# A fused decoder layer on one core: two steps of the attention loop reordered, experts' loads and scatters released differently

## What is computed

```
x = x + attention(layernorm(x))       # rmsnorm * norm_w; 16 heads of 64, causal softmax, sigmoid gate per head, out projection
x = x + retention(layernorm(x), ctx)  # 16 heads of 8: q from x, k = v = ctx, position-rotated, decay mask, no softmax
x = x + experts(layernorm(x))         # 12 experts, top 3 per token, softmax over the 3 logits
                                      # h = gelu(x Wup + bup), 128 -> 512; y = h Wdown + bdown, 512 -> 128
```

## Time and profile before

| | |
|---|---|
| median of 3 runs | 562.97 us (560.76 to 564.37) |
| profiled execution, its own time | 557.62 us |
| its span in the trace | 555.8 us |
| PE busy | 482.0 us, 87% |
| DVE busy | 393.8 us, 71% |
| ACT busy | 340.4 us, 61% |
| POOL busy | 281.2 us, 51% |
| chain that ended last | PE 46%, DVE 19%, issue 10%, ACT 10%, unknown 5% |

### The profile page before, as it was taken

One profiled execution on the slowest core, in us unless ns is written; L12 is line 12 of the kernel. 1 busy time (PEld: TensorE's weight loads), 2 busy tenths in 40 slices (PEclk: granted clock), 3 DMA queues, 4 the chain that ended last, 5 costly groups with the idle time before them and its releaser, 6 DMA issues.

```text
span 555.8 us, 12676 instructions
## 1 busy us (share of the span) xinstructions
PE 482.0 (87%) x3683; PEld 397.1 (71%) x3683; DVE 393.8 (71%) x1324; ACT 340.4 (61%) x1012; POOL 281.2 (51%) x432
## 2 busy tenths in 40 slices
PE   2799999989998998998998999687975899999990
PEld 1567777776785885786677678456665899988880
DVE  4665668878877987887887888776983555445546
ACT  3568766766865865875776686253462666666650
POOL 3400033584375286278258447722748575565554
PEclk9989999999999999999999999778978799999996
DMA  8200000010010000000000001056554687776676
GB/s 269 83 2 1 1 2 2 1 38 0 0 33 5 0 24 14 0 14 24 0 9 29 0 0 39 1 157 174 162 111 138 184 219 214 204 190 197 186 203 153
DMA packets 58196, 42.87 MB, mean 77 GB/s; under 512 B 5059, under 2 KB 51447, under 8 KB 58160
## 3 DMA queue, kind: packets, MB, share of 16 engines
q1 hardware_dynamic: 53904, 35.42, 23.6%
q0 software_dynamic: 3824, 6.49, 3.6%
q10 hardware_dynamic: 432, 0.53, 0.4%
HBM read 31.70 MB, written 12.16 MB: 79 GB/s over the span
## 4 chain that ended last, share of the span: by engine, by line
PE 46%; DVE 19%; issue 10%; ACT 10%; another core or an unknown queue 5%; POOL 4%; SPq 3%; DMA 1%; DVEq 0%; ACTq 0%; POOLq 0%
PE zb L740 8%; PE sc L779 6%; PE ob L808 5%; PE xb L857 4%; PE xb L882 3%; PE tb_a L740 2%; PE ob L994 2%; ACT pT L613 2%; ACT p_sb L606 2%; PE tb_b L740 2%; PE tb_a L792 2%; PE tb_b L792 2%; PE sc L773 2%; PE zb L994 2%
## 5 line engine op out<-in xcount | busy, mean ns | idle before, releaser
L486 POOL TENSOR_TENSOR spare_p<-tri 128x1 f32<-128x1 f32 x94 | 26.6, 283 | 121.2 <-DVE xn L1187 67.0
L597 ACT ACTIVATE qk<-zb 128x512 f32<-128x512 f32 x64 | 38.2, 597 | 74.9 <-PE zb L740 74.9
L563 POOL DMA_INDIRECT results_by_token<-y_sb,row_i x70 | 69.9, 998 | 22.0 <-issue 19.9
L604 ACT ACTIVATE p_sb<-sc,nmx 128x128 f32<-128x128 f32 x128 | 47.0, 367 | 29.5 <-DVE nmx L1106 29.1
L779 PE MATMUL sc<-qk 64*128 64x256 f32 (+1 forms) x512 | 61.9, 362 | 0.2 <-ACT qk L597 0.2
L606 ACT ACTIVATE p_sb<-sc,nmx 128x256 f32<-128x256 f32 x128 | 61.0, 476 | 0.0
L779 PEld LDWEIGHTS sc<-qk 64*128 64x128 f32 x512 | 46.0, 194 | 16.3 <-issue 10.4
L508 POOL DMA_INDIRECT tokens_by_expert<-packed,slot_i x48 | 52.9, 1103 | 8.5 <-issue 7.5
L808 PE MATMUL ob<-pT,v_sb 128*64 128x256 f32 (+1 forms) x512 | 56.4, 342 | 0.9 <-DVE oT L1124 0.9
L1124 DVE TENSOR_TENSOR oT<-ob,pT 128x256 f32<-128x256 f32 x64 | 26.9, 420 | 36.8 <-PE ob L808 25.4
L808 PEld LDWEIGHTS ob<-pT,v_sb 128*64 128x64 f32 x512 | 31.4, 137 | 19.8 <-issue 8.8
(11 more groups left out here) (272 smaller groups left out, 1446.1 us busy)
## 6 DMA issues: line engine op xcount, KB each, us to landing
wup_sb<-in_L_ffn_Wup SPq DMA_DIRECT2D x35, 256.0 KB
wdn_sb<-in_L_ffn_Wdown SPq DMA_DIRECT2D x35, 256.0 KB
xg<-tokens_by_expert SPq DMA_DIRECT2D x35, 130.0 KB
tokens_by_expert<-padding SPq DMA_DIRECT2D x12, 260.0 KB
results_by_token<-y_sb,row_i POOLq DMA_INDIRECT x70
wkv_sb<-in_L_attn_Wkv SPq DMA_DIRECT2D x2, 512.0 KB, 6.4
ctx_b<-in_ctx SPq DMA_DIRECT2D x8, 128.0 KB
out<-x_all SPq DMA_DIRECT2D x4, 256.0 KB, 2.3
```

The lines of the kernel that those rows point to most:

```text
L563: pool.indirect_dma_start(out=ys, out_offset=bass.IndirectOffsetOnAxis(ap=row_i[:, u, a:a + 1], axis=0), in_=y_sb[:, u, a, :], in_offset=None,
L597: act.activation(qk[:, :, :].rearrange("p h j -> p (h j)"), zb[:, :], ACT.Copy).then_inc(a_qk, 1)
L604: act.activation(p_sb[:, w, h, 0:P], sc[:, k, S:S + P], ACT.Exp, bias=nmx[:, w, 0, n:n + 1], accum_out=total[:, w, 0, h:h + 1])
```

## The change

Four edits that touch different engines:

1. **PE, step 3.** `x_T(nxt)`, with its wait for `a_qk`, stands ahead of `weigh` instead of behind it.
2. **DVE, steps 4 to 6.** `ratio(cur, 5)` moves from the head of step 6 to the end of step 5, with nothing between the two places but the start of the next step; `deviation` moves from step 4 to behind it. So `deviation` (12 instructions) now stands between `ratio(5)` and `maxima(6)`, and no longer between the second `read_state` of step 4 and `ratio(4)`.
3. **Experts' loads.** Up weights and tokens of tile n wait for a new semaphore `f_row`, which says that tile n - 6 has been rounded and that its rows and weights have been copied (one more DVE instruction per tile copies the two weight columns to `weight`). The down weights wait for `f_dn` of tile n - 6, have a semaphore of their own (`ld_d`, for which `down` waits), and are started last of the three.
4. **POOL, last batches.** The scatters of tiles 0 and 1 move ahead of the last dispatch, between the sends of batch 6; one send of batch 6 moves ahead of `retained(7, 0)` and one ahead of `queries(7)`; the pacing instructions between these sends go.

```diff
@@ sp, load(n)
                 if n >= DEPTH:
-                    sp.wait_ge(f_y, n - DEPTH + 1)
+                    sp.wait_ge(f_row, n - DEPTH + 1)
...
                 sp.dma_start(wup_sb[:, u, :], f_wup[bass.ds(e, 1)].rearrange("a p n -> p (a n)")).then_inc(ld_e[u], 16)
-                sp.dma_start(wdn_sb[:, u, :, :], dn_v[bass.ds(e, 1)].rearrange("a p c d -> p (a c) d")).then_inc(ld_e[u], 16)
...
                 sp.dma_start(xg[:, u, :, :], xs[bass.ds(r, SLOTS), :].rearrange("(a p) w -> p a w", p=P)).then_inc(ld_e[u], 16)
+                if n >= DEPTH:
+                    sp.wait_ge(f_dn, n - DEPTH + 1)
+                sp.dma_start(wdn_sb[:, u, :, :], dn_v[bass.ds(e, 1)].rearrange("a p c d -> p (a c) d")).then_inc(ld_d[u], 16)
@@ gpsimd, after pack(B - 2)
-            def pace_last(n):
-                if n == 2:
-                    queries(B - 1)
-                    retained(B - 1, 0)
-                if n == 5:
-                    keep(B - 1)
-            dispatch(B - 2, pace_last)
-            pack(B - 1)
-            dispatch(B - 1)
-            for n in range(TILES):
+            begin(B - 2)
+            for n in range(3):
+                send(B - 2, n)
+            queries(B - 1)
+            send(B - 2, 3)
+            retained(B - 1, 0)
+            scatter(0)
+            send(B - 2, 4)
+            keep(B - 1)
+            send(B - 2, 5)
+            scatter(1)
+            pack(B - 1)
+            dispatch(B - 1)
+            for n in range(2, TILES):
+                scatter(n)
@@ tensor, step
-                if (w := lagged(cur, prev, s, 2)) and (cur is not None or s < 2):
-                    weigh(*w)
                 if s == 3 and nxt is not None:
                     pe.wait_ge(a_qk, at(cur, PAIRS, s + 2))
                     x_T(nxt)
+                if (w := lagged(cur, prev, s, 2)) and (cur is not None or s < 2):
+                    weigh(*w)
@@ tensor, down(n)
+                pe.wait_ge(ld_d[u], (n // DEPTH + 1) * 16)
@@ vector, step
-                if (w := lagged(cur, prev, s, 1)) and (s != 2 if cur is not None else s < 1):
+                if (w := lagged(cur, prev, s, 1)) and (s not in (2, 6) if cur is not None else s < 1):
                     ratio(*w, link)
...
                     if s in (4, 5):
                         read_state(prev, s - 4, 1)
-                    if s == 4:
+                if cur is not None and s == 5:
+                    ratio(cur, 5, link)
+                if prev is not None:
+                    if s == 5:
                         deviation(link, brs)
@@ vector, tokens(n) and results(n)
                 dve.tensor_copy(row_i[:, u, :], xg[:, u, :, D].bitcast(I32))
+                dve.tensor_copy(weight[:, u, :], xg[:, u, :, D + 1]).then_inc(f_row, 1)
...
-                    ins = dve.tensor_scalar(y_sb[:, u, a, :], y_sb[:, u, a, :], xg[:, u, a, D + 1:D + 2], None, ALU.mult)
+                    ins = dve.tensor_scalar(y_sb[:, u, a, :], y_sb[:, u, a, :], weight[:, u, a:a + 1], None, ALU.mult)
```

More of the change, by code:

```diff
@@ L209, in decoder @@
         row_i = sb("row_i", [P, DEPTH, HALVES], I32)
+        weight = sb("weight", [P, DEPTH, HALVES])
         bdn_sb = sb("bdn_sb", [P, E, D])
@@ L261, in decoder @@
         ld_e = [sem(f"ld_e{u}") for u in range(DEPTH)]
+        ld_d = [sem(f"ld_d{u}") for u in range(DEPTH)]
         scattered = [sem(f"scattered{u}") for u in range(DEPTH)]
@@ L280, in decoder @@
         pe_CNT, v_hit, v_filled, v_slot, v_pad, v_first, v_plan, v_fin = (sem(n) for n in ("pe_CNT", "v_hit", "v_filled", "v_slot", "v_pad", "v_first", "v_plan", "v_fin"))
+        f_row = sem("f_row")
         f_T, f_hi, f_w, f_xg, f_up, f_gelu, f_dn, f_y, f_out = (
@@ L495, in pack, with send, begin @@
                 ins.then_inc(p_pack, 1)
-            def dispatch(b, pace=None):
+            def send(b, n):
+                t, k = divmod(n, TOPK)
+                pool.indirect_dma_start(
+                    out=xs, out_offset=bass.IndirectOffsetOnAxis(ap=slot_i[:, t, k:k + 1], axis=0),
+                    in_=packed[:, t, k, :], in_offset=None).then_inc(dispatched, 16)
+            def begin(b):
                 if b == B - 1:
@@ L502, in dispatch @@
                 carry(1)
+            def dispatch(b, pace=None):
+                begin(b)
                 for n in range(T * TOPK):
@@ L506, in dispatch @@
                         carry(3 + n)
-                    t, k = divmod(n, TOPK)
-                    pool.indirect_dma_start(
-                        out=xs, out_offset=bass.IndirectOffsetOnAxis(ap=slot_i[:, t, k:k + 1], axis=0),
-                        in_=packed[:, t, k, :], in_offset=None).then_inc(dispatched, 16)
+                    send(b, n)
             def keep(b):
@@ L544, in _, with scatter @@
             pack(B - 2)
-            def pace_last(n):
-                if n == 2:
-                    queries(B - 1)
-                    retained(B - 1, 0)
-                if n == 5:
-                    keep(B - 1)
-            dispatch(B - 2, pace_last)
-            pack(B - 1)
-            dispatch(B - 1)
-            for n in range(TILES):
+            def scatter(n):
                 u = n % DEPTH
@@ L698, in up_high @@
                 u = n % DEPTH
-                act.wait_ge(ld_e[u], (n // DEPTH + 1) * 48)
+                act.wait_ge(ld_e[u], (n // DEPTH + 1) * 32)
                 act.activation(wup_hi[:, n % 2, :], wup_sb[:, u, :], ACT.Copy).then_inc(f_w, 1)
@@ L966, in turn_tokens @@
                 u = n % DEPTH
-                pe.wait_ge(ld_e[u], (n // DEPTH + 1) * 48)
+                pe.wait_ge(ld_e[u], (n // DEPTH + 1) * 32)
                 wait(pe, f_xg, n)
```

## The result

| | before | after |
|---|---|---|
| median, 10 runs each on one chip | 560.44 us (558.21 to 564.42) | 567.05 us (562.30 to 569.12) |
| profiled execution, own time | 557.62 us | 567.07 us |
| span | 555.8 us | 565.3 us |
| DVE in the chain that ended last | 19% | 27% |

The ratio of after to before is 1.0096, with an interval from 1.0055 to 1.0137: slower by 3 to 8 us. The ratios in this document are taken over the runs and are not quotients of the medians. They leave out runs over 1.5% above the fastest of their kernel (three runs of root_step3, none of any other kernel).

A forecast was written before the change was run, and what follows sets the result against it. PE, busy 42.3 of 45 us, was taken to bound the loop, with DVE level at step 7. Terms 6.6 - 0.4 - 0.5 + 0.6 - 2.3 = + 4.0 us on 562.97 gave 567 us, range 556 to 573.

The forecast's parts named there:

- The place of the root, and the new wait: Root's 12 `deviation` instructions ahead of `maxima(6)`: all on the path, + 2.7 us; PE waits about 2 us at `scores(7)`.
- + 1.1 us per iteration: Loop: moved root costs + 1.65 us, earlier x wins 0.55; net + 1.1 per iteration, 45.9 us instead of 44.8.
- + 6.6 us: Whole loop: six iterations at + 1.1 us each; bounds - 1.0 to + 11.7 us.
- x gives 0.55: Step 3: turning x ahead of the product with V wins 0.55 us per iteration of PE's 1.49 us wait; bounds 0 to 1.49.
- Which price the root keeps beside POOL: Root's new place, beside POOL's additions: 3.00 us if contended, 2.37 undisturbed; midpoint 2.7 taken.
- Batch 7, "- 0.5": Last batch: root leaves POOL's two products, the plan slides under them; - 0.5 us, bound one 1.86 us stall either way.
- Experts, "+ 0.6 - 2.3" and "steady 0": Experts' start: four more DVE copies cost + 0.6 us, earlier loads and scatters win 2.3; steady tiles unchanged, 0.
- C: Rival: root in front of `maxima(6)` keeps 3.00 us and x gives nothing; loop + 11.7, 572 us; chance 0.2.
- A: Rival: PE's results become visible on time, earlier x wins all 1.49 us per iteration; 559.4 us; chance 0.25.
- B: Rival: experts gain most, steady stretch loses its 9% idle time (- 5.5 us), start wins 5.6; 558.2 us; chance 0.15.
- The page on the ends of products: Matmul ends are estimated: PE really worked until about 257, its idle time before 258.07 isn't real, x gives 0.
- The tie at the masks: Start of step 7: PE and DVE reach the masks of `scores(7)` together, so whatever delays `maxima(6)` delays PE.

The follow-up runs named there:

- root_step3: Kernel before with all 12 `deviation` instructions (the root) moved forward into step 3, ahead of `scale_out(1)`; ratio 1.0206 to the kernel before.
- fill10: Changed kernel with 10 more mask products inside PE's wait at `scores(7)`, into a bank overwritten anyway; 547.04 us, ratio 1.0139 to the kernel before.
- split_after: Changed kernel with the root cut in two, six instructions in step 4 and six in step 5; 532.52 us, ratio 0.9880 to the kernel before.
- split_before: Kernel before with the root cut in two, six instructions ahead of step 4's first read and six in step 5; 530.72 us, ratio 0.9851.
- x_alone: Kernel before with only `x_T(nxt)` moved ahead of `weigh` in step 3; 539.84 us, ratio 1.0024.
- root_alone: Kernel before with only the root and `ratio(5)` moved behind the last read of step 5; 550.95 us, ratio 1.0232.
- loads_alone: Kernel before with only the experts' loads changed, scatters as before; ratio 1.0009.
- changed_again: The changed kernel itself, run on another chip; 550.74 us, ratio 1.0214 to the kernel before there.
- experts_alone: Kernel before with only the experts' loads changed and the scatters of tiles 0 and 1 between the sends; ratio 1.0021.
- the cut root: Kernels with the root's 12 instructions cut in two or three pieces under waits in steps 4 and 5; ratios 0.9851, 0.9831 and 0.9880 to the kernel before.
- fill: Changed kernel with 16 more mask products ahead of the first mask of `scores(7)`; 549.6 us, ratio 1.0202 to the kernel before.
- root_behind_maxima: Kernel before with the whole root in step 6, behind `maxima(6)` and ahead of the second residual; 541.12 us, ratio 1.0033.

## Why the prediction came out, point by point

- **The place of the root, and the new wait.** Right. All 12 instructions are on the path, 2.65 us against the forecast's 2.7; PE's wait for `rg` is gone; the new wait is at the second mask of `scores(7)`, behind exponentials that wait for DVE (about 2 us forecast, 2.53 measured).
- **The size of edits 1 and 2, "+ 1.1 us per iteration".** Right only where the clock holds: 45.94 us against 45.9. The step that failed is the sum of the loop, "+ 6.6 us", bounds to + 11.7: it priced a wait of some 2 us at its own length. The runs show + 1.4 to + 1.5 more behind each wait after which the clock falls to 1.2 GHz, four times in the profiled execution: + 12.5, outside my bounds. Removing 1.1 us of the emptiness (fill10) removed it. The trace of before had no wait of that length in the loop, but it had the price of the clock, in the stretch at 0.72; I used it for the experts only. It also had a fall behind shorter waits, in batch 7, where two of 1.81 and 1.88 us follow within 3.2 us. The second of them, and PE's clock right behind it (0.50 in the last columns):

```profile
352.16 0.80 PE L882 MATMUL xb<-kv_hi,tri_r 128*128 128x512 f32 x1 [1.88 <-DVE prod L1169]
354.00:356.00 2.00, 2.00 (x10) 1.50 (x11) 1.79 (x8) 0.00 (x0) 1.66 (x4) 0.50 0.00 0
```

- **"x gives 0.55".** Wrong on the chips of the experiments: 0 (44.39 against 44.32, and nothing in split_after). The wait of 1.49 us that it was to shorten hung on signals that came late by "remote" and is 0.22 us where these don't. My own reason against it, that the read waits for POOL's queries, is what these traces show (1.28 us). On the first chip the parts of the 1.1 us weren't run, so an x that wins up to half a microsecond there is not excluded.
- **Which price the root keeps beside POOL.** In its new place its instructions take the 0.16 to 0.17 us of the undisturbed row, with one exception of 0.36. Beside POOL's two-input products and additions single ones take more: 0.48 and 0.58 us in split_before's first half, 0.72 once in its second. The Trainium skill's rule (GPSIMD Engine Reference, Specifications), that GpSimd's SBUF interfaces are shared with VectorE, agrees with these. It names VectorE instructions with two SBUF inputs, which the one of 0.72 is, or in a 2-port mode; those of 0.48, 0.58 and 0.36 have one tensor as input, and no run here shows their mode. By the prediction's reading of it the new place would have cost 3.00 us, and that did not come: of its 2.65 us all but 0.3 are undisturbed.
- **Batch 0.** Forecast - 0.4, measured - 0.1, in line with x giving nothing.
- **Batch 7, "- 0.5".** Measured - 3.4, outside its bounds of 1.86 either way. The bounds took one stall of the root under POOL's products. The trace of before has two, one behind the other, and PE waits 3.71 us for the `rg` that comes after them. In the trace of after that wait is 1.84 us, though the plan has stalls of its own there (1.39 and 1.81 us). Before twice, then after:

```profile
357.74 1.87 DVE L1046 SCALAR_TENSOR_TENSOR nwt<-nwa,brs 128x2 f32<-128x2 f32 x1
363.12 0.47 PE L797 MATMUL tb_a<-ident,rg 128*128 128x128 f32 x1 [3.71 <-DVE rg L1119]
```

```profile
372.71 0.33 PE L815 MATMUL tb_a<-ident,rg 128*128 128x128 f32 x1 [1.84 <-DVE rg L1138]
```

  Edit 2 alone moves the same wait from 5.07 us (x_alone) to 1.30 (root_alone), and the stretch from 85.2 to 82.9 us, with one fall of the clock from the loop's last wait inside it. Against this stands what the forecast left out, the new wait of 2.44 us at the masks of this batch too. The mean clock of the stretch is 0.86 before (340 to 401) and 0.91 after (351 to 410). So a gain by edit 2 is likely here. Its size isn't shown: loads_alone, with the old root, has 83.5 us, and the 3.4 aren't taken apart.
- **Experts, "+ 0.6 - 2.3" and "steady 0".** The start's size came out not far off (- 2.7 against - 1.7), and DVE's wait at `row_i` is gone as forecast. The mechanism isn't borne out: on chips without the "remote" waits edits 3 and 4 win nothing, and tile 8 comes 1.9 us later. The steady tiles then cost 2.3 us more. The window of after on the first chip, against 85.00 us of PE work in 85 in changed_again's of 444 to 529, shows that this, too, is the first chip's:

```profile
457.00:542.00 85.00, 77.62 (x656) 75.58 (x656) 44.21 (x154) 55.21 (x135) 47.55 (x66) 1.00 0.66 189
```

  After its start every second tile took 4.3 us instead of 3.43, before from tile 19 on and after from tile 12 on. This rhythm goes with "remote" waits of DVE's bias addition, one in every second tile, from 469.84 on before and from 458.95 on after. Two of before:

```profile
477.59 0.42 DVE L1394 TENSOR_TENSOR y_sb<-ob,bdn_sb 128x256 f32<-128x256 f32 x1 [3.39 <-remote]
485.34 0.42 DVE L1394 TENSOR_TENSOR y_sb<-ob,bdn_sb 128x256 f32<-128x256 f32 x1 [3.67 <-remote]
```

  Why they set in, and earlier, is open.
- **The rivals.** C had the right place (the root in front of `maxima(6)`), and the loop came out near its price of + 11.7, but by other terms: the root took 2.65 us and not 3.00, and the clock, which C didn't have, made up the rest. Its 572 us was missed because of the last batch and the start. On the other chips, where less is given back, the whole is 550.74 - 538.64 = + 12.1 us, above C's + 9.1. A (PE's results on time) is refuted in its consequence: where they are on time, edit 1 wins nothing, since then there is no wait to win. B didn't come: the steady part lost. Its premise holds on the first chip alone, since on the others PE has no idle time there to win.
- **The page on the ends of products.** The Trainium skill (Perfetto Trace Analysis, Tensor Engine Instruction) says that the end of a matmul is estimated and its semaphore follows the real one. `oT` waits 2.26 us by "remote" on one chip, and on the others, in kernels with the same loop (experts_alone, loads_alone), it starts without a wait. This agrees with the page insofar as the recorded end doesn't show when the result can be read; whether the product or its signal is late, no trace shows. That x gives 0 was measured where nothing is late, so it doesn't bear on the page.
- **The tie at the masks** had a slack of 0.2 to 0.3 us on the other chips: with a perfect tie 2.65 - 0.77 - 0.29 = 1.6 us per iteration would be lost where the clock holds, 1.3 were.

## What to carry to other kernels

Price a new wait of the matmul engine not at its length alone but with the clock behind it: here a wait of 2.5 us cost up to 1.5 more, ten useless products inside it were a gain, and the same work moved to where it made waits of 1.3 us cost half. When a chain of small instructions has to move, lay it in pieces under waits that exist, each piece no longer than its wait, and look at what runs beside it on the engine that shares the memory. A wait whose releaser the profile can't name is not slack to be counted on: here it was a matter of the chip. Of the two plans that counted on it, x ahead of V gave nothing and the root in step 3 lost 2% on chips without it; whether they pay where it exists wasn't tried. And look at what is written out behind a loop: of the 9 to 11 us that the cut root won in the traces, 3.4 to 5.7 lay in the last batch and its tail.

## What the runs showed of the hardware

- The granted clock fell to 1.2 GHz behind four of six waits of 2.52 to 2.54 us in the trace of after, and again behind four of six in root_alone and in changed_again. In root_step3 it fell behind three of five waits of 2.2 us. It never fell in the loop behind waits of 1.44 to 1.45 us (fill10, six), 0.79 (fill), 1.31 (root_behind_maxima) or 1.47 to 1.56 (split_before, split_after). In batch 7 it fell behind two waits of 1.8 and 1.9 us within 3.2 us (0.50 from 354 to 356 in the trace of before). The same wait in the same loop may or may not cost it. The Trainium skill (TensorE: Matmul & The Clock Gate, The HAM clock gate) says that the check of the activity runs freely and doesn't start with the kernel; that one of two equal waits costs and the other doesn't agrees with this. Its rule of thumb for idle gaps (HAM oscillation) would have let waits of this length pass, and the windows at 0.50 show otherwise.
- One kernel takes 560 us on one chip and 538 to 540 on two others, though the instructions are recorded with the same durations (`oT` 0.42 us, eight products with V 0.87). I found three differences: 44.77 against 44.3 us per iteration, 34.6 against 27.8 to 28.7 us from the last `x2b` to tile 8, and steady tiles at 3.43 and 4.3 us in turn against 3.43 throughout. In all three places the trace of the first chip has "remote" waits and the others have none.
- A change measured at + 0.96% on one chip was + 2.1% on another.
